# Value pieces leave the normalisation, the attention entry and two SyncE queues are reordered, and ScalarE spreads the values of a chunk

## The reference

```python
xn = _layernorm(x)
q, k, v = silu(xn @ Wq.T), silu(xn @ Wk.T), xn @ Wv.T
log_f = log_sigmoid(xn @ Wf.T + delta)            # one decay per token and head
lf = cumsum(log_f, within a chunk of 128 tokens)
# per chunk, qb, kb, vb, lb of one head:
o_inter = (qb * exp(lb)) @ S
A = (qb @ kb.T) * exp(where(mask, lb_i - lb_j, -inf))
o = o_inter + A @ vb
S = exp(tot) * S + (kb * exp(tot - lb)).T @ vb    # tot = lb of the last token
attn = (o * rsqrt(mean(o * o) + 1e-6) * norm_weight) @ Wo.T
# experts: gates over expert 0 and the best of experts 1 to 7
h = silu(flat_x @ W1[e].T) * (flat_x @ W3[e].T)
out = out + gates[:, e] * (h @ W2[e].T)
x + attn + out
```

## Time and profile before

| | us |
|---|---|
| median of 3 runs | 374.39 (373.97 to 377.28) |
| the profiled execution, its own time | 372.6 |
| its span, first to last instruction | 370.8 |
| PE busy | 323.7 (87%) |
| DVE busy | 261.9 (71%) |
| POOL busy | 243.6 (66%) |
| ACT busy | 220.2 (59%) |

### The profile page before, as it was taken

One profiled execution on the slowest core, in us unless ns is written; L12 is line 12 of the kernel. 1 busy time (PEld: TensorE's weight loads), 2 busy tenths in 40 slices (PEclk: granted clock), 3 DMA queues, 4 the chain that ended last, 5 costly groups with the idle time before them and its releaser, 6 DMA issues.

```text
span 370.8 us, 14229 instructions
## 1 busy us (share of the span) xinstructions
PE 323.7 (87%) x5226; PEld 267.8 (72%) x5226; DVE 261.9 (71%) x579; ACT 220.2 (59%) x474; POOL 243.6 (66%) x292
## 2 busy tenths in 40 slices
PE   0799995599989989999979999998599997999970
PEld 0699663266656656777769999997399996999960
DVE  5961681259989978778838899888167775777740
ACT  1455795546656655555556777665177776777750
POOL 5432060669998989999949999800057766667773
PEclk9999999579999999999999999999699999999996
DMA  8696036412354311222260111111224444344332
GB/s 231 245 265 232 3 99 179 122 38 72 105 143 142 99 53 46 69 70 59 57 229 22 45 28 29 42 28 30 57 45 63 63 61 65 52 64 65 43 36 22
DMA packets 45961, 31.68 MB, mean 85 GB/s; under 512 B 10950, under 2 KB 43590, under 8 KB 45606
## 3 DMA queue, kind: packets, MB, share of 16 engines
q1 hardware_dynamic: 37974, 22.75, 22.3%
q0 software_dynamic: 7504, 7.95, 12.2%
q10 hardware_dynamic: 432, 0.28, 0.3%
HBM read 18.17 MB, written 12.79 MB: 84 GB/s over the span
## 4 chain that ended last, share of the span: by engine, by line
PE 65%; POOL 14%; issue 6%; ACT 4%; DMA 3%; DVE 1%; SPq 1%; POOLq 0%; ACTq 0%; DVEq 0%
PE PS L995 62%; POOL xsort L470 3%; POOL out L555 3%; POOL C L519 3%; DMA C<-k_scr 1%; POOL C L511 1%; PE PS L1167 1%; PE PS L1036 1%; POOL C L529 1%; POOL C L524 1%; SPq L372 1%; DMA lb_scr<-C 1%; DMA k_scr<-C 1%; POOL C L494 1%; POOL C L491 1%
## 5 line engine op out<-in xcount | busy, mean ns | idle before, releaser
L555 POOL DMA_INDIRECT out<-F,ids x44 | 68.3, 1552 | 57.0 <-DVE ids L932 34.4
L995 PE MATMUL PS<-C 64*32 64x64 f32 (+3 forms) x2816 | 85.1, 270 | 11.5 <-ACT Z L605 4.0
L995 PEld LDWEIGHTS PS<-C 64*32 64x32 f32 (+3 forms) x2816 | 58.2, 120 | 37.3 <-issue 18.2
L942 DVE TENSOR_TENSOR F<-F,PS 128x512 f32<-128x512 f32 x76 | 51.7, 686 | 24.8 <-PE PS L995 15.3
L995 PE MATMUL PS<-C,W 128*128 128x256 f16 (+1 forms) x530 | 63.8, 278 | 3.8 <-DVE C L936 3.7
L702 ACT ACTIVATE F<-PS 128x512 f32<-128x512 f32 x76 | 45.3, 598 | 27.8 <-PE PS L995 21.3
L995 PEld LDWEIGHTS PS<-C,W 128*128 (+1 forms) x530 | 52.7, 100 | 11.7 <-issue 4.6
L948 DVE TENSOR_TENSOR F<-F 128x512 f16<-128x512 f32 x76 | 52.1, 701 | 4.0 <-ACT F L707 1.2
L707 ACT ACTIVATE F<-F 128x512 f16<-128x512 f32 x76 | 47.5, 630 | 11.2 <-DVE F L942 8.4
L658 ACT ACTIVATE C<-PS 128x512 f32<-128x512 f32 x64 | 38.1, 596 | 26.4 <-PE PS L995 22.1
L995 PE MATMUL PS<-xh,W 128*128 (+1 forms) x256 | 44.7, 273 | 1.7 <-DVE F L942 1.3
(11 more groups left out here) (132 smaller groups left out, 572.6 us busy)
## 6 DMA issues: line engine op xcount, KB each, us to landing
F<-w SPq DMA_DIRECT2D x8, 512.0 KB, 5.3
xsort<-C POOLq DMA_DIRECT2D x1, 2860.0 KB, 9.0
C<-xsort SPq DMA_DIRECT2D x22, 130.0 KB
x_sb<-x SPq DMA_DIRECT2D x8, 256.0 KB, 5.6
k_scr<-C SPq DMA_DIRECT2D x8, 256.0 KB, 2.9
C<-k_scr SPq DMA_DIRECT2D x32, 64.0 KB
C<-elb_scr SPq DMA_DIRECT2D x32, 64.0 KB, 2.2
out<-x_sb SPq DMA_DIRECT2D x16, 128.0 KB, 1.8
```

The costliest lines, as they stand in the source:

```text
L555: pool.indirect_dma_start(out, bass.IndirectOffsetOnAxis(ap=ids[:, k:k + 1], axis=0), ysb[:, n % 2, t, :], None, compute_op=ALU.add).then_ ...
L942: dve.tensor_tensor(silu[:, half, :], silu[:, half, :], PS[:, 3 + 4 * half, :], ALU.mult).then_inc(S["f_h"], 1)
L995: return pe.matmul(out_, lhsT, rhs, start=start, stop=stop)
```

## The change

- PE makes no value pieces during normalisation. Six of them (`NEARLY = 6`) come right after the last logits, with q and k of group 0, then the decay sums; the values of groups 6 and 7 are made inside step 0 of the chunk loop, into banks 5 and 6, and drained by DVE (`late_v`); u(0) waits for that. ACT's `values` are placed around the exponentials of the decays and the router.
- SP stores the keys of groups 2 and 3 before it waits for the exponents' stores and loads the rows.
- The growth factors of chunks 0 and 1 come from a product of PE with a new constant `grow` and an exp of ACT out of PSUM (`elb_first`); the exp of all of them, its store and with it SP's wait for that store move into step 0.
- In the chunk loop the spreading of the values moves from POOL to ACT, between the copy of o and the first exp. POOL waits for the table's `sdec` before, not after, an always-met wait.
- ACT loads the table of Silu in step 31 instead of at the first Silu of the experts.
- SP loads the sorted rows of blocks 2 and 3 before the stores of the last two blocks of expert 0.
- The zeroing of the first state moves up in DVE's list.

```diff
@@ -60 +60 @@
 for _name, _n in [("ident", P), ("hmask", H), ("hsel", HQ),
-          ("rank", P), ("ones", P), ("cum", P), ("suffix", P), ("expand", P), ("cmask", CG),
+          ("rank", P), ("ones", P), ("cum", P), ("suffix", P), ("expand", P), ("grow", P), ("cmask", CG),
...
@@ -89 +89 @@
     put("expand", (k % H == head_of(m)))
+    put("grow", (k < H) & (k == head_of(m)))
...
@@ -293 +294 @@
 NLBDMA = 3
-NPIECE = 4 * NGRP
+NEARLY = 6
+NPIECE = NEARLY + 3 * NGRP
...
@@ -309 +311 @@
-    return 4 + i % 4 if i < NGRP else 3 + (i - NGRP) % 5
+    return 4 + i if i < 4 else 3 + (i + 2) % 5
...
+def late_bank(g):
...
+    return 5 + g - NEARLY
...
-    return NGRP + 3 * g + t
+    return NEARLY + 3 * g + t
...
@@ -389 +395 @@
     sp.wait_ge(S["init_out"], 16)
-    for p in range(3):
-        store_exponents(p)
-        if p < 2:
-            store_keys(p)
+    store_exponents(0)
+    store_keys(0)
+    store_exponents(1)
+    store_keys(1)
+    store_keys(2)
+    store_exponents(2)
+    store_keys(3)
...
     load_keys(chunk(0, 0), 0)
-    for g in range(2, NGRP):
+    for g in range(4, NGRP):
...
@@ -406 +415 @@
     sp.wait_ge(S["elb_out"], 16)
-    for b in range(2):
-        load_growth(chunk(0, b), b)
...
@@ -427 +434 @@
-    def load_rows(i):
+    def load_rows(n, u):
+        slots = bass.ds(at(sp, n * BW), BW)
+        wait(sp, S["xs_ps"], n - 1)
+        wait(sp, S["id_copied"], n - 1)
+        sp.dma_start(xrow[:, u], xsort[slots, :].rearrange("(t p) r -> p t r", p=P)
+                     ).then_inc(S[f"xrow_in{u}"], 16)
...
+    def load_pair(i):
         for u in range(2):
-            n = 2 * i + u
-            slots = bass.ds(at(sp, n * BW), BW)
-            wait(sp, S["xs_ps"], n - 1)
-            wait(sp, S["id_copied"], n - 1)
-            sp.dma_start(xrow[:, u], xsort[slots, :].rearrange("(t p) r -> p t r", p=P)
-                         ).then_inc(S[f"xrow_in{u}"], 16)
...
-    load_rows(0)
+            load_rows(2 * i + u, u)
...
+    load_pair(0)
...
     for n in range(N0):
+        if n >= N0 - 2:
+            load_rows(n - N0 + 4, n % 2)
...
                      x_sb[:, n * BT:(n + 1) * BT, :]).then_inc(S["base_out"], 16)
-    loop(sp, NBLK // 2, load_rows, peel=0, start=1)
+    loop(sp, NBLK // 2, load_pair, peel=0, start=2)
...
@@ -507 +518 @@
         wait(pool, S["pe_i"], n - 1)
-        pool.wait_ge(S[f"elb_in{b}"], 16 * (n // 2) + 16)
+        if n < 2:
+            pool.wait_ge(S["elb_first"], 1)
+        else:
+            pool.wait_ge(S[f"elb_in{b}"], 16 * (n // 2))
...
@@ -518 +532 @@
                            cc("hsel").unsqueeze(2).broadcast_to([P, HQ, P]), ALU.mult).then_inc(S["pool_qb"], 1)
-        wait(pool, S["pe_u"], n - 1)
...
             pool.wait_ge(S["sdec"], 1)
+        wait(pool, S["pe_u"], n - 1)
...
                            ).then_inc(S["pool_kd"], 1)
-        wait(pool, S["pe_av"], n - 1)
-        pool.tensor_copy(v_of(slice(0, P), b), v_sb[:, c, :].rearrange("p (q h e) -> p q h e", q=HQ, h=HQ)
-                         ).then_inc(S["pool_v"], 1)
...
@@ -590 +601 @@
             act.activation(wqh[:], wraw.rearrange("p w d -> p (w d)"), ACT.Copy, scale=WS).then_inc(S["wq_hi"], 1)
-        if g >= 4:
-            values(g - 4)
...
@@ -604 +613 @@
-    values(4)
-    values(5)
...
     act.activation(ze, ze, ACT.Exp).then_inc(S["forget_exp"], 1)
-    values(6)
-    values(7)
+    values(0)
+    values(1)
...
     act.activation(ze, ze, ACT.Ln, bias=one).then_inc(S["forget_ln"], 1)
+    for g in range(2, NEARLY):
+        values(g)
...
@@ -628 +637 @@
-    act.wait_ge(S["tot_in"], 1)
-    act.wait_ge(S["lb_rest"], 1)
-    act.wait_ge(S["lbT_sb"], 1)
-    act.activation(lbT, lbT, ACT.Exp).then_inc(S["elb_exp"], 1)
...
@@ -663 +668 @@
             if has(0):
+                if n == 3:
+                    act.wait_ge(S["late_v"], NGRP - NEARLY)
+                wait(act, S["pe_av"], n - 1)
+                act.activation(v_of(slice(0, P), b),
+                               v_sb[:, chunk(i, b), :].rearrange("p (q h e) -> p q h e", q=HQ, h=HQ), ACT.Copy
+                               ).then_inc(S["act_v"], 1)
                 decays(0)
+            if known and n == 0:
+                act.wait_ge(S["grow_ps"], 1)
+                act.activation(elb_now.rearrange("p b t -> p (b t)"), PS[:, 7, 0:2 * P], ACT.Exp
+                               ).then_inc(S["elb_first"], 1)
...
@@ -673 +688 @@
                 act.activation(dec[:], dec[:], ACT.Exp).then_inc(S["dec"], 1)
+                act.wait_ge(S["tot_in"], 1)
+                act.wait_ge(S["lb_rest"], 1)
+                act.wait_ge(S["lbT_sb"], 1)
+                act.activation(lbT, lbT, ACT.Exp).then_inc(S["elb_exp"], 1)
+            if known and n == NCH - 1:
+                act.activation(ssq[:, 0:1], one, ACT.Silu)
...
@@ -683 +704 @@
     act.wait_ge(S["blocks_known"], 1)
+    act.wait_ge(S["blocks_zero"], 1)
...
@@ -871 +893 @@
+    link(dve.memset(state[:, :, 0, :], 0.0), "state_zero")
...
     dve.tensor_copy(dec[:], PS[:, 0, 0:NCH * NS]).then_inc(S["tot_sb"], 1)
+    for g in range(NEARLY, NGRP):
+        dve.wait_ge(S["late_piece"], g - NEARLY + 1)
+        dve.tensor_scalar(v_sb[:, g * GRP:(g + 1) * GRP, :].rearrange("p c d -> p (c d)"),
+                          PS[:, late_bank(g), :], 1.0 / WS, None, ALU.mult).then_inc(S["late_v"], 1)
...
     dve.wait_ge(S["init_out"], 16)
-    link(dve.memset(state[:, :, 0, :], 0.0), "state_zero")
...
@@ -1006 +1032 @@
+    def by_tokens(g, bank, t):
+        w = slice(t * D, (t + 1) * D)
+        for j in range(GRP):
+            tok = slice((g * GRP + j) * P, (g * GRP + j + 1) * P)
+            last = split_product(PS[:, bank, j * D:(j + 1) * D], xh[:, tok], xl[:, tok], wqh[:, w], wql[:, w])
+        return last
...
         bank = piece_bank(i)
-        if i == NGRP:
+        if i == 8:
             pe.wait_ge(S["router_in"], 1)
-        wait(pe, S["drained"], i - 3 if i < NGRP else i - 4)
-        g, t = (i, 2) if i < NGRP else divmod(i - NGRP, 3)
-        if i < NGRP or t < 2:
-            pe.wait_ge(S["xl_ready"], g + 1)
-        if i >= NGRP and t < 2:
+        wait(pe, S["drained"], i - 3 if i < 8 else i - 4)
+        g, t = (i, 2) if i < NEARLY else divmod(i - NEARLY, 3)
+        pe.wait_ge(S["xl_ready"], g + 1)
+        if i >= NEARLY and t < 2:
...
         else:
-            w = slice(2 * D, 3 * D) if i < NGRP else slice(D, 2 * D)
-            for j in range(GRP):
-                tok = slice((g * GRP + j) * P, (g * GRP + j + 1) * P)
-                last = split_product(PS[:, bank, j * D:(j + 1) * D], xh[:, tok], xl[:, tok], wqh[:, w], wql[:, w])
+            last = by_tokens(g, bank, 2 if i < NEARLY else 1)
...
@@ -1037 +1066 @@
             route(g - 1)
-        if g == 3:
-            pe.wait_ge(S["wq_lo"], 1)
-        if g >= 3:
-            project(g - 3)
     route(NGRP - 1)
-    for i in range(NGRP - 3, 13):
+    pe.wait_ge(S["wq_lo"], 1)
+    for i in range(8):
...
     mm(PS[:, 1, :], cc("suffix"), lf).then_inc(S["suffix_ps"], 1)
+    project(8)
...
     last.then_inc(S["lbT_ps"], 1)
-    project(13)
+    project(9)
...
     mm(PS[:, 2, NCH * R:2 * NCH * R], cc("ones"), flat).then_inc(S["rank_ps"], 1)
-    for i in range(14, 18):
+    for i in range(10, 14):
...
     mm(PS[:, 0, 0:NCH * NS], cc("expand"), tot).then_inc(S["tot_ps"], 1)
-    for i in range(18, NPIECE):
+    for i in range(14, NPIECE):
...
@@ -1116 +1143 @@
+            if known and n == 0:
+                for k in range(2):
+                    g = chunk(0, k) // CG
+                    last = mm(PS[:, 7, k * P:(k + 1) * P], cc("grow"), lbT[:, g * P:(g + 1) * P])
+                last.then_inc(S["grow_ps"], 1)
+                for g in range(NEARLY, NGRP):
+                    by_tokens(g, late_bank(g), 2).then_inc(S["late_piece"], 1)
+                pe.wait_ge(S["late_v"], NGRP - NEARLY)
             pe.wait_ge(S["pool_kd"], n + 1)
-            pe.wait_ge(S["pool_v"], n + 1)
+            pe.wait_ge(S["act_v"], n + 1)
...
```

## The result

The changed kernel took 439.05 us (median of 4 runs, 437.48 to 441.57), the kernel before 374.32 us beside it: a ratio of 1.17, 95% interval 1.163 to 1.180. The forecast was 356.5 us. The profiled execution took 441.57 us, its span is 439.8 us, against 372.6 and 370.8 us before.

The account below looks back on a forecast made before the run. PE, busy for 87% of the span, was taken as the bound where it stands still or runs slowly. Terms -8.3 - 3.0 - 0.5 - 6.1 = -17.9 us took 372.6 to 354.7, 356.5 us as median; range 351 to 363.

Parts of the forecast that it names:

- Early chunks: Early chunk-loop steps: POOL loses 0.34 us of spreading, 0.2 us gained for some 15 steps, -3.0 us (0 to -4.8).
- Late chunks: Late chunk-loop steps: no gain, PE's list is the bound; ACT's spreading just in time, 0 to +0.1 us a step.
- PE falls to the half clock: Rival, entry: clock falls while PE waits for chunk 2's exponents, costing some 5 us; 361.5 us, chance 0.10.
- the wait for exponents: Entry: PE reaches chunk 2's exponents at 66.5 and stands 2.6 us until their load lands at 69.1.
- Slower than before: Rival, chunk loop: ACT's spreading takes over 0.8 us, so u waits in all 32 steps; 378 us, chance 0.02.
- The groups of the normalisation: Normalisation: without value pieces, groups 2.48 us apart instead of 3.69, putting group 7's transposes at 27.3, 4.8 us earlier.
- ACT copies the sums: Way to the decay sums: ACT's copy at 41.3 against 45.97, 4.7 us gained.
- no drain waits for a store of keys: Entry: ACT's 4.26 us stall before a drain of keys goes, as group 2's keys are stored earlier.
- the scores of chunk 0: Entry: they begin at 57.9 instead of 64.94, 7.0 us earlier.
- The entry: From the start to chunk 1's state products: 71.1 against 79.43, -8.3 us, bounds -11 and -5.
- The table load: Into the experts: the 1.28 us Silu load moves to step 31, delaying a copy of o; -0.5 us (0 to -1.3).
- The sorted rows: Start of the sorted blocks: earlier loads remove PE's 4.54 us wait and the half clock behind it; -6.1 us (-5.5 to -6.7).

Follow-up runs that it names:

- e4: The kernel before with one part alone: SP loads the rows of blocks 2 and 3 ahead of its last two stores of the first expert; 367.03 us, 0.973.
- e6: The changed kernel with one wait more: POOL starts a chunk's scatter only after PE ends that step's products of scores and values; 367.01 us, 0.979.
- e8: The changed kernel with one part undone: POOL spreads the values again instead of ACT; 362.62 us, 0.963.
- e13: The changed kernel with POOL's scatter of a chunk waiting until PE has ended the scores of that chunk; 359.01 us, 0.951.
- e15: The kernel before with ACT spreading the values and the scatter waiting for the scores of its chunk; 373.16 us, 0.988.
- e3: The kernel before with one part alone: ACT spreads the values of a chunk instead of POOL; 454.60 us, 1.200.
- e1: The changed kernel with 64 dense fp16 matmuls, results unused, in step 2 of the chunk loop behind the exponents; 441.85 us, 1.176.
- e2: The changed kernel with 25 fp16 matmuls, results unused, where PE stood idle in steps 0 and 1; 421.42 us, 1.115.
- e14: The changed kernel with the scatter left in place but of 32 bytes a row instead of 520, to its own array; 439.40 us, 1.166.
- e7: The kernel before with the scatter waiting for the same step's state products, so it lies over the 64 products; POOL still spreads; 452.13 us, 1.20.
- e16: The changed kernel with the scatter waiting for its chunk's scores and 25 unused fp16 matmuls in the entry's idle times; 355.69 us, 0.944.
- e11: The changed kernel with POOL's 32 indirect DMAs replaced by plain ones of the same bytes from the same queue; 358.76 us, 0.948.
- e10: The changed kernel with POOL's 32 scatters replaced by an in-place multiplication of about 1 us without a DMA; 357.83 us, 0.947.
- e5: The changed kernel without POOL's 32 indirect DMAs of rows to xsort and without waits for them; 354.31 us, 0.945.

## Why the prediction was wrong, step by step

**What failed: "Early chunks" and "Late chunks".** They had the loop gain 3.0 us, and it lost 81.7. They took POOL's copy of the values as 0.34 us of work that goes and asked what becomes the bound next. They did not ask what moves up. POOL's list had been full, and that had kept the scatter ahead of the 64 products. Without the copy POOL is early, waits for the state products at its product of the queries, and is released just so that the scatter starts 0.8 us after the 64 products begin, in every step but the first and the last three, which have no scatter there: the wait locks it in that place. The prediction went through ACT's and DVE's lists behind the moved copy, but not through POOL's, from which it was taken.

The price could have been seen in the trace of before, in the one step in which the scatter, from 140.21 to 141.24, ran past the start of the products (the 64 begin at 141.06):

```profile
140.21 1.03 POOL L470 DMA_INDIRECT xsort<-rows,slot_i  x1 [0.16 <-issue]
...
140.50 1.71 PE L995 MATMUL PS<-C 128*128 128x64 f32 x68
...
142.50 0.28 ACT L663 ACTIVATE C<-PS 128x128 f32<-128x128 f32 x1 [0.93 <-PE PS L995]
```

1.71 us instead of 1.42 for the issue, and 2.00 to the copy of o, for 0.18 us of overlap.

**What failed too: the rival "PE falls to the half clock".** It had the fall in the right part of the kernel, though PE got it at 64.31, after idle times of 0.78 and 0.78 us and in the midst of one of 1.10, and not at the wait for exponents:

```profile
61.63 0.49 PE L1021 MATMUL PS<-C 64*128 64x128 f32 x4 [0.78 <-DVE Z L901]
62.05 0.39 PE L1021 MATMUL PS<-dR,dL 118*128 118x512 bf16 x1
63.22 0.38 PE L1021 MATMUL PS<-dR,dL 118*128 118x512 bf16 x1 [0.78 <-ACT C L663]
64.69 1.89 PE L1021 MATMUL PS<-C 32*64 32x256 f32 x20 [1.10 <-DVE C L923]
...
73.05 2.18 PE L1021 MATMUL PS<-C 128*128 128x64 f32 x67
```

Its price, some 5 us, supposed that the clock comes back by itself as it did before. It does where the products run freely: 6.8 to 24 us later in e4 to e6, e8 to e13 and e15. With the scatter on the products it did not in 201 us here and in 212 in e3; where it was brought up (e1) or kept up (e2), and where it had come back by itself before the scatter met the products (e14, 72.2), it fell again in the loop. In e7 it took 17, 61 and 82 us to come back, and fell again after 10, 20 and 14. So the scatter does not forbid the rise; it makes the fall likely and the rise late. That PE's standing behind the slow products is what lowers the clock fits all these runs and is not shown by itself. At half clock a step is 6.4 us long, against 5.6 with free products (e4, 79.85 to 85.47).

**Where the 81.7 us went**, worked out from e2: its five steps at full clock took 4.72 us against 3.54 on average before, 1.2 us in each of 31 steps, 37 us; the rest, 45 us, is the half clock, which in no trace with free products stayed for over 24 us at a time. The split goes by the order: at half clock the slow products cost only the 0.8 us between 5.6 and 6.4.

**The loss and its rival.** "Slower than before" had been given 0.02, by another mechanism, a spreading on ACT that takes over 0.8 us. It takes 0.30 us (0.31 was assumed), and with the scatter moved u begins 0.62 us after the scores in nearly every step of e13 at full clock, as in the late steps before. The loss has nothing to do with that rival.

**What was right.** The groups of the normalisation are 2.5 us apart (17.59, 20.06, 22.60, 25.08 and 27.53; 27.3 was forecast for the last), ACT copies the sums at 41.50 (41.3), no drain waits for a store of keys, the scores of chunk 0 begin at 58.17 (57.9), u at 61.63 (61.3), the store of the growth factors goes out at 63.76 (63.4), and the exponents of chunk 2 run at 69.37 (69.1). The last is luck: PE comes there without idle time, since its own work at half clock fills the 2.6 us. The wait that was forecast is seen in e16, 1.42 us long and ended by the load at 69.15. The entry is worth 6.4 us in the changed kernel, since it ends at half clock, 7.1 in e13, and 8.3 us in e16, at 71.16: the -8.3 of the sum, there with fillers in PE's idle times.

The gain in an early step was sized well, once the scatter is out of the way: e13's take 3.35 to 3.49 us, and 3.47 was forecast; low parts of the weights last 0.68 to 0.95 us there instead of 0.68 to 1.20. The loop as a whole is 4.2 us shorter than before in e16, where -3.0 was forecast, but 2.2 us longer in e13, which lost the clock once in it. e15, the spreading alone, gains 1.2% with an interval of 0.1 to 2.3%.

The table load behaved as put: it makes ACT's copy of o late in step 31 (PE waits 1.07 us for it instead of 0.57, e13), and from the first expert to the rows of block 0 it takes 59.52 us instead of 60.41, together -0.4 us against the -0.5 forecast.

The sorted rows were sized too low: -7.6 us in e4, where -6.1 (-5.5 to -6.7) was forecast. The step without a late load takes 5.3 us (332.89 to 338.20), not the 6.73 taken from another boundary:

```profile
332.89 0.39 PE L1202 MATMUL PS<-kept_cst,C 128*128 128x128 f32 x2
334.10 2.81 PE L1021 MATMUL PS<-C,W 128*128 128x256 f16 x24 [0.82 <-ACT C L714]
336.75 1.61 PE L1021 MATMUL PS<-Z,F 128*128 x24
338.20 0.39 PE L1202 MATMUL PS<-kept_cst,C 128*128 128x128 f32 x2
```

With the scatter moved (e13) the whole change comes to 359.0 us, 0.951 of the kernel before beside it, in the range that was given; without that one wait it is 439. That e13 is so near the forecast is partly luck: against before, its profiled execution has -7.1 us at the entry, +2.2 in the loop and -8.6 from the first expert to block 3, where -8.3, -3.0 and -6.6 were forecast.

## To carry to other kernels

When work is taken off an engine, follow what its queue does next, and where that now falls against the other engines: a list that was full had an order, and the order can be worth more than the work. Write that order down as a wait, if something depends on it. And price a lower clock by whether the code that follows can lift it again, not by how long the last fall lasted.

## What the runs showed of the hardware

POOL's indirect DMA holds up PE's small fp32 products. With 1.0 to 1.5 us of scatter over them, ACT's copy of o, which waits for the last of them, comes 1.6 to 1.8 us after the scatter's start (e2 1.62, e14 1.70, e7 1.75, the changed kernel 1.84), with 32 bytes a row as with 520, and no later where the scatter itself lasts 1.47 us instead of 0.99. From the first state product that is 3.04 us instead of 1.45 at full clock and 3.62 instead of 2.25 at half clock. In e7 PE is seen to stop issuing; in e2 and e14 it had issued all of them by the start of the scatter, and their end still came only behind it. A plain DMA of the same bytes (e11), or an arithmetic operation of POOL (e10), does nothing of the kind. Where the scatter lay over exponents, output and state products only, as in the late steps before, a step took 3.35 to 3.46 us, as in e5 without a scatter. The Trainium skill, SBUF — State Buffer, Who interferes with whom, has PE never wait for another engine's access to SBUF, with the pair shared by DVE and GpSimd as the one place of contention. For DVE the runs agree in part: in e7 an operation with two SBUF inputs, begun 0.35 us into the scatter, took 1.90 us instead of 0.35, but in e2 the low part of the weights, also with two, begun 0.25 us into it (85.52), kept its 0.68. For PE they do not agree, or PE waits for something else than SBUF, which stays open.

A loop in which PE is busy for 93% of the time (187.92 of 201.39 us) stayed at the 1.2 GHz level for 201 us. It rose 1.3 us after the dense fp16 products behind it began, and 12.7 us after the first of its three last steps, which have no scatter; no run tells the two apart.

The kernel before is not safe from this either: one of its 40 timed runs took 433.62 us at a mean granted clock of 0.753, against 0.93 to 0.97 in the others for which it is recorded. It left no trace, so whether its scatter had slipped onto the products is not known.
